# A hand-ordered Mamba, experts and attention kernel: new order times in the state loops, first convolution tap on ScalarE, a shorter row split

## The chip, the cores and the metric

The kernel runs on one NeuronCore of a Trainium2 chip. The metric is the time of one execution in microseconds (us) on the device; shorter is better. The time before is the median of three runs. Four layers are computed in one launch on 4 batches of 1024 tokens of 128 channels. The engines are PE (TensorE), DVE (VectorE), ACT (ScalarE), POOL (GpSimd) and SP, which here only issues transfers.

## What is computed

The reference, cut to the layers that the change touches. Two more layers follow, a differential attention and a layer of soft experts.

```python
x = x + _layernorm(_mamba_forward(_layernorm(x), ...))
x = x + _layernorm(_L0_ffn_ref(_layernorm(x), ...))
x = x + _layernorm(_L1_attn_ref(_layernorm(x), ...))
x = x + _layernorm(_L1_ffn_ref(_layernorm(x), ...))

def _mamba_forward(x, ...):                 # d_exp = 256, n = 16 states, dt rank 8
    u, z = split(x @ W_in.T)
    uc = silu(conv(u, taps=3) + conv_b)
    B_ssm, C_ssm, dt = split(uc @ W_xproj.T)
    delta = softplus(dt @ W_dt.T + b_dt)
    h = exp(delta * A) * h + (delta * uc) * B_ssm      # over time, for each of 16 states
    y = sum_n h * C_ssm + uc * D
    return (y * silu(z)) @ W_out.T

def _L0_ffn_ref(x, ...):                    # 8 experts, top 2, and one shared expert
    h = gelu(x @ W1[e] + b1[e]);  y = h @ W2[e] + b2[e]
    return sum over the top two of w * y  +  gelu(x @ sW1 + sb1) @ sW2 + sb2
```

## The kernel before

Every engine's program is written out in full, with semaphores between engines. Each engine runs its instructions strictly in the order in which they are written. That order is made by `weave`: each stream of work (state loop, front, middle, back, expert layer) is a Python generator that yields a planned time ahead of each piece, and the piece with the smallest time is emitted next. The times stand in tables (`IN_AT` for the front of a batch, `OUT_AT` for its back, `F_AT` for its expert layer) and in numbers in the loop functions. They set the order and nothing else; no instruction waits for a time.

Work on the 1024 tokens of a batch lies transposed: 256 inner channels as two halves c = 0, 1 of 128 partitions, time along the free dimension.

**The state loop** (`loop_dve`, `loop_act`, `loop_pe`, `loop_pool`) has 16 iterations per batch, one for each state n. This text calls iteration n of batch b "b.n". In one iteration:

- PE spreads row n of B over all partitions (L548 into `ps0`), later row n of C (into `ps1`).
- ACT makes `exp(delta * A)` for both halves (L451).
- DVE does six instructions of 1024 columns: two products with the B row (L328), the scans of c = 1 and of c = 0 (L334), two products with the C row (L340). The scan of c = 1 has one input in PSUM; that of c = 0 has both inputs in SBUF (`BIG`).
- POOL adds the two products to `yy` (L423, both inputs in SBUF). It starts when the first L340 is done.

**The front** of batch b+1 runs inside the loop of batch b: statistics (L306, L310), normalization (L315, eight instructions), transposes (L561) and the input product (L568) on PE, copies to `up` on ACT (L464), the convolution on DVE for each half (first tap L356, two more taps L360), SiLU on ACT (L469), the projection (L575, L473), the split of the projected rows into three bf16 parts (L366 to L376), softplus (L382, L384, L389, L392 with exponentials and logarithms on ACT), and `du` (L397). **The back** of batch b (gate L406, output product L603, statistics, normalization, addition to X by POOL at L437) runs inside the loop of batch b+1, and so does its **expert layer**: statistics and normalization, transposes (L768), the low part of the input (L659), gate logits (L757 to L759 with the small `gw`), top two (L634 to L668), weights (L671 to L681), and then 18 expert steps (9 experts on two halves of the tokens). A step is four groups "up" of three matmuls (L757 to L759) with a GELU each on ACT (L744), then "down" (L828, 32 records of 128 columns; with a bias product L826 for the shared expert), whose result DVE weighs and sums (L696, four instructions; `PLAN`'s shared expert is copied by ACT, L752). For batches 0 to 2 all "down" results go through one PSUM bank, so the next "down" waits until the last sum is done. The loop of batch 3 has no front in it; the back and the expert layer of batch 3 come after all loops.

ACT holds one table set of functions at a time: between the exponentials of the loop and the GELUs it runs an ACT_TABLE_LOAD.

After that come a barrier, the attention, a barrier, and the soft experts. The constants are loaded by SP at the start; ACT and DVE wait for all of them together (semaphore `s_c`).

## Time and profile before

| | us |
|---|---|
| median of 3 runs | 3073.71 (3073.69 to 3076.74) |
| the profiled execution | 3073.01 |
| its span, first to last instruction | 3070.9 |
| mean granted TensorE clock | 0.873 |
| busy: PE / DVE / ACT / POOL | 2391.0 / 2202.3 / 1696.2 / 1448.7 |
| start of the loop of batch 0, 1, 2, 3 (first L328) | 72.79 / 270.61 / 513.97 / 766.73 |
| end of the last loop; transposes of the last expert layer | 987.42 / 1027.21 |

The page gives busy shares over the whole span. To read a stage, one takes the start of an instruction that marks it (here the first L328 of each loop) and asks for the busy time of each engine between two such marks. A row "engine line <- engine line" names who ended a wait. In the rows that list groups of instructions, the mean length of one stands behind the busy time: the same instruction with two lengths has been held up in one of them.

### The profile page before, as it was taken

To read this page: it belongs to the slowest core of one execution; us is meant where nothing else is said; L and a number is where in the kernel's file an instruction comes from. 1 tells how busy PE (TensorE), PEld (TensorE's weight loads), DVE (VectorE), ACT (ScalarE), POOL (GpSimd) and SP (SyncE) were. 2 spreads that over 40 slices of the span, in tenths; PEclk is the share of its full clock that TensorE was granted. 3 is DMA by queue.
4 is the path that set the end of the run, shared out by engine and by line. 5 is a ranking of instruction groups with operands and counts; after the bars stand their busy time and mean duration, and the time that the engine had idled before them with its cause. 6 is when DMAs were issued, how large, how long until landed. Compare 5 with 4: busy or idle time off the path is not lost.

```text
span 3070.9 us, 42340 instructions
## 1 busy us (share of the span) xinstructions
PE 2391.0 (78%) x15570; PEld 1711.5 (56%) x15570; DVE 2202.3 (72%) x3693; ACT 1696.2 (55%) x2621; POOL 1448.7 (47%) x1343
## 2 busy tenths in 40 slices
PE   2333579388488794999999999999999478767987
PEld 0101256156256572777677777777777356745675
DVE  5999999989986314888788878887888543354334
ACT  5333476376474342878777877787777224222322
POOL 0434323433433102655866676667567541564156
PEclk7555699698798896999999999999999789887988
DMA  3000000000000001101000000000000100000000
GB/s 103 0 0 0 1 1 1 0 1 1 0 1 1 1 1 40 26 24 29 21 23 22 22 22 22 22 22 21 22 22 1 42 1 1 1 14 1 1 1 14
DMA packets 32031, 42.04 MB, mean 14 GB/s; under 512 B 8897, under 2 KB 18130, under 8 KB 31442
## 3 DMA queue, kind: packets, MB, share of 16 engines
...
## 4 chain that ended last, share of the span: by engine, by line
PE 49%; DVE 24%; issue 12%; POOL 9%; ACT 5%; SPq 1%; DMA 0%; POOLq 0%; DVEq 0%; ACTq 0%
PE ps L1073 10%; PE ps L1051 6%; PE ps L1062 6%; PE ps L828 5%; DVE MA L1209 3%; DVE lnb L315 2%; DVE BIG L340 2%; PE ps L757 2%; PE ps L1842 2%; PE ps L1033 2%; PE ps L759 2%; PE ps L758 2%; DVE BIG L334 2%; PE ps L1784 1%; DVE ps L328 1%
## 5 line engine op out<-in xcount | busy, mean ns | idle before, releaser
L1209 DVE TENSOR_REDUCE MA<-ps 128x1 f32<-128x1024 f32 x512 | 623.3, 1221 | 191.4 <-PE ps L1051 178.6
L423 POOL TENSOR_TENSOR MA<-MA,BIG 128x1024 f32<-128x1024 f32 x128 | 309.3, 2438 | 590.4 <-DVE BIG L340 559.1
L1073 PE MATMUL ps<-MA,WB 128*64 128x128 f32 x4096 | 504.4, 277 | 0.0
L1073 PEld LDWEIGHTS ps<-MA,WB 128*64 128x64 f32 x4096 | 442.6, 137 | 88.9 <-issue 87.9
L1051 PE MATMUL ps<-BIG 96*128 96x512 f16 x1024 | 313.8, 388 | 13.6 <-ACT WB L1136 5.0
L1136 ACT ACTIVATE WB<-ps,MA 128x1024 f32<-128x1024 f32 x206 | 229.7, 1115 | 149.2 <-DVE MA L1209 149.2
L828 PEld LDWEIGHTS ps<-WB,HR 128*128 128x128 f32 x2304 | 285.5, 199 | 32.5 <-issue 16.9
L828 PE MATMUL ps<-WB,HR 128*128 128x128 f32 x2304 | 295.5, 285 | 9.0 <-DVE acc L696 9.0
L744 ACT ACTIVATE HR<-ps,b 128x512 f32<-128x512 f32 x288 | 191.2, 687 | 174.1 <-PE ps L759 173.3
L1143 ACT ACTIVATE MA<-ps 128x1024 f32<-128x1024 f32 x256 | 259.9, 1015 | 5.0 <-PE ps L1062 5.0
L1605 POOL TENSOR_TENSOR BIG<-MA,BIG 128x512 f32<-128x512 f32 x128 | 132.2, 1049 | 232.3 <-PE ps L1828 74.5
L1266 POOL TENSOR_TENSOR MA<-MA 128x2 f32<-128x2 f32 x128 | 25.2, 197 | 366.7 <-DVE MA L1213 366.7
L451 ACT ACTIVATE BIG<-MA,aneg 128x1024 f32<-128x1024 f32 x128 | 141.3, 1143 | 100.7 <-DVE BIG L334 98.8
L1136 ACT ACTIVATE MA<-ps,MA 128x1024 f32<-128x1024 f32 x153 | 170.7, 1116 | 45.7 <-DVE MA L1209 45.5
L696 DVE SCALAR_TENSOR_TENSOR acc<-ps,g,acc 128x128 f32<-128x128 f32 x256 | 71.7, 342 | 159.7 <-PE ps L828 159.6
L548 PE MATMUL ps<-bc,sel 96*128 96x512 bf16 x128 | 54.8, 524 | 162.2 <-DVE BIG L334 104.4
L1062 PE MATMUL ps<-ident,WB 128*128 128x128 f32 x1232 | 166.7, 279 | 5.4 <-POOL WB L1278 2.6
L1062 PEld LDWEIGHTS ps<-ident,WB 128*128 128x128 f32 x1232 | 144.7, 144 | 44.0 <-DVE WB L1218 10.9
L757 PE MATMUL ps<-xT,WB 128*128 128x512 f16 x288 | 119.2, 414 | 48.4 <-ACT HR L744 42.9
L334 DVE TENSOR_TENSOR_SCAN BIG<-BIG,ps 128x1024 f32<-128x1024 f32 x64 | 146.2, 2284 | 5.3
L340 DVE TENSOR_TENSOR BIG<-BIG,ps 128x1024 f32<-128x1024 f32 x128 | 149.0, 1205 | 0.1
L334 DVE TENSOR_TENSOR_SCAN BIG<-BIG 128x1024 f32<-128x1024 f32 x64 | 146.5, 2289 | 0.0
(306 smaller groups left out, 5262.3 us busy)
## 6 DMA issues: line engine op xcount, KB each, us to landing
...
```

Of the source, the lines that this page charges most:

```text
L334: e.tensor_tensor_scan(db[k][c], da[k][c], db[k][c] if c == 0 else ps[0][:, :], 0.0, ALU.mult, ALU.add).then_inc(*v_mscan.up(b, n, c))
L340: e.tensor_tensor(db[k][c], db[k][c], ps[1][:, :], ALU.mult).then_inc(*v_mth.up(b, n, c))
L423: e.tensor_tensor(yy[:, c, :], yy[:, c, :], db[n % 2][c], ALU.add).then_inc(*p_my.up(b, n, c))
L744: e.activation(hr[(4 * k + f) % 8], bank[4 + f % 2], ACT.Gelu, bias=small["b1"][:, PLAN[k][1], f:f + 1], scale=BACK).then_inc(*a_fg.up(b, ...
L757: e.matmul(o, w[0], x[0], start=first, stop=False)
L828: i = e.matmul(o, hr[(4 * kk + f) % 8][:, 128 * j:128 * j + 128], w2[:, x, f, :], start=f == 0 and x != 8, stop=f == 3)
L1051: x = e.matmul(ps[s][:, 512 * h:512 * h + 512], stack[q % 2][0:96, 0, 2 * pp + s, 128 * i:128 * i + 128], stack[q % 2][0:96, 1, 2 * pp + s ...
L1062: x = e.transpose(ps[2][:, 128 * k:128 * k + 128], P_of(n, 0)[:, 128 * k:128 * k + 128], ident[:, :])
L1073: x = e.matmul(bank[6][64 * pp:64 * pp + 64, 0:128], V[(4 * b + g) % 2][:, k, 64 * pp:64 * pp + 64], DT[n % 2][:, 128 * k:128 * k + 128], ...
L1136: e.activation(P_of(n, s), ps[s][:, :], ACT.Exp, bias=L[:, 2 * s + pp:2 * s + pp + 1], scale=1.0, accum_out=L[:, 4 + 2 * s + pp:5 + 2 * s ...
L1143: e.activation(DT[n % 2], ps[2][:, :], ACT.Copy, scale=1.0).then_inc(*a_at.up(n))
L1209: e.tensor_reduce(L_of(n)[:, c:c + 1], ps[s][:, :], AX, ALU.max, negate=True).then_inc(*v_amx.up(n, s))
```

## The change

1. New numbers in the tables and in the loop functions (now `LOOP_AT`, `F_AT0`, `F_AT2`, `F_AT3`). They reorder the streams on all engines up to the end of the first expert layer.
2. The first tap of the convolution, with the bias, goes from DVE (L356) to ACT (an Identity activation with a scale and a bias for each partition), after the last copy to `up`.
3. The split of the projected rows writes straight into the rows that PE reads; each part is made on fewer partitions. Four DVE instructions take the place of six.
4. The load of `lnp` (four transfers) goes from the start to the beginning of the attention.
5. A way of weighing the experts on ACT and POOL is added, but `WEIGHTED = []` leaves it unused, so the sums stay on DVE.

```diff
-N_PERIOD, M_PERIOD, M_FIRST = 14.0, 224.0, 56.0
+N_PERIOD, M_PERIOD, M_FIRST = 13.11, 209.76, 56.0
+WEIGHTED = []
...
-IN_AT = {"stats": slot(4), "norm": slot(5), "tr": 82.5, "u": 87, "conv0": slot(6), "conv1": slot(7), "silu": 111.5,
+IN_AT = {"stats": 59.8, "norm": 72, "tr": 75, "u": 79.5, "tap0": 90.3, "tap1": 88, "conv0": 84.9, "conv1": 98,
...
+LOOP_AT = {"tb": 0.04, "scan1": 2.4, "scan0": 4.95, "th": 7.2, "add": 9.57, "da": 0.1, "rows0": 5.5, "rows1": 10.88,
+           "z": 20.8, "zK": 1.85, "za": 0.98}
...
-        for i in range(4):
-            consts += [(lnp[:, i, :], d["lnp"][i:i + 1, :].partition_broadcast(128)),
-                       (lam[:, i, :], d["lam"][i:i + 1, :].partition_broadcast(128))]
+        consts += [(lam[:, i, :], d["lam"][i:i + 1, :].partition_broadcast(128)) for i in range(4)]
...
             for c in range(2):
                 yield in_at(b, f"conv{c}")
-                e.wait_ge(*a_m.at("u", b, c, 1))
-                if c == b == 0:
-                    e.wait_ge(*p_const.at("pad"))
-                e.tensor_scalar(cv[c], u[:, c, 0:1024], cw[:, c, 0:1], cb[:, c:c + 1], ALU.mult, ALU.add).then_inc(
-                    *dve_own.up())
                 for k in (1, 2):
-                    e.wait_ge(*dve_own.now())
+                    if k == 1:
+                        e.wait_ge(*a_mtap.at(b, c))
+                    else:
+                        e.wait_ge(*dve_own.now())
...
-            e.tensor_copy(bc[0], r).then_inc(*dve_own.up())
+            e.tensor_copy(hi, r[0:96, :]).then_inc(*dve_own.up())
             e.wait_ge(*dve_own.now())
-            e.tensor_tensor(r, r, bc[0], ALU.subtract).then_inc(*dve_own.up())
+            e.tensor_tensor(r[0:64, :], r[0:64, :], hi[0:64, :], ALU.subtract).then_inc(*dve_own.up())
             e.wait_ge(*dve_own.now())
             yield in_at(b, "bc2")
-            e.tensor_copy(bc[1], r).then_inc(*dve_own.up())
+            e.tensor_copy(hi[0:64, :], r[0:64, :]).then_inc(*dve_own.up())
             e.wait_ge(*dve_own.now())
-            e.tensor_tensor(hi, r, bc[1], ALU.subtract).then_inc(*dve_own.up())
-            e.wait_ge(*dve_own.now())
-            e.tensor_copy(hi[32:64, :], bc[1][32:64, :])
-            e.tensor_copy(hi[0:32, :], bc[0][0:32, :]).then_inc(*v_mbc.up(b))
+            e.tensor_tensor(hi[0:32, :], r[0:32, :], hi[0:32, :], ALU.subtract).then_inc(*v_mbc.up(b))
...
+            for c in range(2):
+                yield in_at(b, f"tap{c}")
+                for h in range(2):
+                    e.wait_ge(*a_m.at("u", b, c, h))
+                if c == b == 0:
+                    e.wait_ge(*p_const.at("pad"))
+                if c and b:
+                    e.wait_ge(*v_mdl.at(b - 1, 0))
+                e.activation(cv[c], up[b % 2][:, c, 0:1024], ACT.Identity, bias=small["convb"][:, c:c + 1],
+                             scale=small["convw"][:, c, 0:1]).then_inc(*a_mtap.up(b, c))
...
+            for i in range(4):
+                e.dma_start(lnp[:, i, :], d["lnp"][i:i + 1, :].partition_broadcast(128)).then_inc(s_lnp, 16)
```

What the tables do is seen in the order of the instructions. First DVE in iterations 1.6 and 1.7, where the taps of batch 2 are taken. L334 is a scan, L340 the product with the C row, L696 the sum of an expert. The order before:

```order
L334 SCALAR_TENSOR_TENSOR BIG<-BIG 128x1024
L340 TENSOR_TENSOR BIG<-BIG,ps 128x1024 x2
L356 TENSOR_SCALAR lnb<-MA,convw,convb 128x1024
L360 SCALAR_TENSOR_TENSOR lnb<-MA,convw,lnb 128x1024 x2
L328 TENSOR_TENSOR BIG<-MA,ps 128x1024
L328 TENSOR_TENSOR ps<-MA,ps 128x1024
L334 SCALAR_TENSOR_TENSOR BIG<-BIG,ps 128x1024
L334 SCALAR_TENSOR_TENSOR BIG<-BIG 128x1024
L696 SCALAR_TENSOR_TENSOR acc<-ps,g,acc 128x128 x4
L340 TENSOR_TENSOR BIG<-BIG,ps 128x1024 x2
L356 TENSOR_SCALAR BIG<-MA,convw,convb 128x1024
L360 SCALAR_TENSOR_TENSOR BIG<-MA,convw,BIG 128x1024 x2
```

The taps stood behind the pair L340. The same place now, from the normalization in 1.5 on (L316 is L315 of before, L329 is L328, L335 is L334, L341 is L340, L359 is L360, L706 is L696):

```order
L316 TENSOR_SCALAR lnb<-X,st_m 128x128 x8
L341 TENSOR_TENSOR BIG<-BIG,ps 128x1024 x2
L329 TENSOR_TENSOR BIG<-MA,ps 128x1024
L329 TENSOR_TENSOR ps<-MA,ps 128x1024
L335 SCALAR_TENSOR_TENSOR BIG<-BIG,ps 128x1024
L706 SCALAR_TENSOR_TENSOR acc<-ps,g,acc 128x128 x4
L335 SCALAR_TENSOR_TENSOR BIG<-BIG 128x1024
L359 SCALAR_TENSOR_TENSOR lnb<-MA,convw,lnb 128x1024 x2
L341 TENSOR_TENSOR BIG<-BIG,ps 128x1024 x2
L706 SCALAR_TENSOR_TENSOR acc<-ps,g,acc 128x128 x4
```

The normalization and the taps now stand between the second scan and the pair of products; the other pieces of the fronts and backs moved in the same way. Second, ACT at the front of batch 2, where the first tap is now made (L762 is the GELU, L460 the copy to `up`, L470 the tap, L447 the exponentials of the loop):

```order
L447 ACT_TABLE_LOAD
L447 ACTIVATE BIG<-MA,aneg 128x1024 x2
L460 ACTIVATE MA<-ps 128x512 x2
L762 ACT_TABLE_LOAD
L762 ACTIVATE HR<-ps,b 128x512 x2
L460 ACTIVATE MA<-ps 128x512
L762 ACTIVATE HR<-ps,b 128x512 x2
L460 ACTIVATE MA<-ps 128x512
L470 ACTIVATE lnb<-MA,convb,convw 128x1024
L470 ACTIVATE BIG<-MA,convb,convw 128x1024
```

Both taps stand behind all four copies and four GELUs. Third, DVE after the last iteration, from the last pair of products to the transposes of the last expert layer. Before:

```order
L340 TENSOR_TENSOR BIG<-BIG,ps 128x1024 x2
L696 SCALAR_TENSOR_TENSOR acc<-ps,g,acc 128x128 x4
L406 TENSOR_TENSOR MA<-MA 128x1024 x2
L306 BN_STATS st_m<-lnb 128x6 x8
L310 BN_AGGR st_m<-st_m 128x2 x8
L696 SCALAR_TENSOR_TENSOR acc<-ps,g,acc 128x128 x4
L315 TENSOR_SCALAR lnb<-lnb,st_m 128x128 x8
L696 SCALAR_TENSOR_TENSOR acc<-ps,g,acc 128x128 x8
L306 BN_STATS st_f<-acc 128x6 x8
L310 BN_AGGR st_f<-st_f 128x2 x8
L315 TENSOR_SCALAR lnb<-acc,st_f 128x128 x8
L306 BN_STATS st_f<-X 128x6 x8
```

And now (L402 is the gate):

```order
L341 TENSOR_TENSOR BIG<-BIG,ps 128x1024 x2
L706 SCALAR_TENSOR_TENSOR acc<-ps,g,acc 128x128 x4
L402 TENSOR_TENSOR MA<-MA 128x1024 x2
L706 SCALAR_TENSOR_TENSOR acc<-ps,g,acc 128x128 x4
L307 BN_STATS st_f<-acc 128x6 x8
L311 BN_AGGR st_f<-st_f 128x2 x8
L316 TENSOR_SCALAR lnb<-acc,st_f 128x128 x8
L307 BN_STATS st_m<-lnb 128x6 x8
L311 BN_AGGR st_m<-st_m 128x2 x8
L316 TENSOR_SCALAR lnb<-lnb,st_m 128x128 x8
L307 BN_STATS st_f<-X 128x6 x8
```

Two expert sums instead of four stand behind the loop, and the closing of the expert layer of batch 2 stands ahead of the closing of batch 3's Mamba layer.

## Rows read from the trace of the kernel before

**Rows 1.** Stretches (loops 0 to 3, transition): length; PE, PEld, DVE, ACT, POOL busy; clock.
```profile
72.79:270.61 197.82, 61.96 (x102) 13.94 (x102) 194.45 (x143) 68.01 (x70) 76.87 (x33) 0.52 0.00 0
270.61:513.97 243.36, 170.15 (x869) 104.40 (x870) 224.13 (x284) 139.53 (x162) 88.89 (x40) 0.78 0.00 1
513.97:766.73 252.76, 178.32 (x986) 113.67 (x985) 232.36 (x319) 150.93 (x175) 92.17 (x43) 0.83 0.00 1
766.73:987.42 220.69, 161.02 (x946) 106.52 (x945) 187.86 (x269) 123.31 (x143) 86.07 (x41) 0.83 0.00 1
987.42:1027.21 39.79, 21.00 (x155) 16.65 (x154) 20.04 (x90) 6.29 (x10) 14.05 (x10) 0.88 0.00 1
```

**Rows 2.** DVE in order of time: start, length; one bare iteration, 0.0.
```profile
72.79 1.22 DVE L328 TENSOR_TENSOR BIG<-MA,ps 128x1024 f32<-128x1024 f32 x1
...
81.88 1.21 DVE L328 TENSOR_TENSOR BIG<-MA,ps 128x1024 f32<-128x1024 f32 x1
```

**Rows 3.** POOL's adds and what stands beside them on DVE, by time.
```profile
345.35 4.65 POOL L423 TENSOR_TENSOR MA<-MA,BIG 128x1024 f32<-128x1024 f32 x2 [8.38 <-DVE BIG L340]
...
346.32 5.30 DVE L315 TENSOR_SCALAR lnb<-X,st_m 128x128 f32<-128x128 f32 x8
...
286.62 3.57 DVE L334 TENSOR_TENSOR_SCAN BIG<-BIG 128x1024 f32<-128x1024 f32 x1
```

**Rows 4.** DVE by group in the four loops, 73 to 987: busy, mean of one.
```profile
L392 DVE SCALAR_TENSOR_TENSOR MA<-MA,lnb 128x1024 f32<-128x1024 f32 x6 | 19.5, 3254 | 0.2
L315 DVE TENSOR_SCALAR lnb<-X,st_m 128x128 f32<-128x128 f32 x24 | 15.9, 730 | 0.0
L360 DVE SCALAR_TENSOR_TENSOR BIG<-MA,convw,BIG 128x1024 f32<-128x1024 f32 x6 | 13.6, 2270 | 0.2
...
L315 DVE TENSOR_SCALAR lnb<-X,st_f 128x128 f32<-128x128 f32 x24 | 6.4, 339 | 0.0
...
L356 DVE TENSOR_SCALAR BIG<-MA,convw,convb 128x1024 f32<-128x1024 f32 x3 | 5.8, 1934 | 0.0
...
L356 DVE TENSOR_SCALAR lnb<-MA,convw,convb 128x1024 f32<-128x1024 f32 x3 | 2.8, 929 | 7.6 <-ACT MA L464 7.6
...
L375 DVE COPY rows<-bc 32x1024 bf16<-32x1024 bf16 x2 | 0.8, 417 | 0.1
```

**Rows 5.** The same instructions with POOL at rest, DVE before the loops.
```profile
33.74 2.61 DVE L360 SCALAR_TENSOR_TENSOR lnb<-MA,convw,lnb 128x1024 f32<-128x1024 f32 x2
...
69.26 1.22 DVE L392 SCALAR_TENSOR_TENSOR MA<-MA,lnb 128x1024 f32<-128x1024 f32 x1
```

**Rows 6.** DVE's waits in the four loops: total, times, longest.
```profile
DVE acc L696 <- PE ps L828: 50.4, 19, 9.1
DVE lnb L356 <- ACT MA L464: 7.6, 3, 3.6
DVE bc L366 <- ACT lnb L473: 5.2, 3, 2.7
```

**Rows 7.** PE and the pace of the experts, by time.
```profile
407.26 0.38 PE L757 MATMUL ps<-xT,WB 128*128 128x512 f16 x1
407.48 0.38 PE L758 MATMUL ps<-xT,WB 128*128 128x512 f16 x1
...
410.16 3.73 PE L828 MATMUL ps<-WB,HR 128*128 128x128 f32 x32
...
937.90 2.08 PE L828 MATMUL ps<-WB,HR 128*128 128x128 f32 x8
...
1068.38 1.12 DVE L696 SCALAR_TENSOR_TENSOR acc<-ps,g,acc 128x128 f32<-128x128 f32 x4 [5.34 <-PE ps L828]
```

**Rows 8.** ACT by group in the loops.
```profile
L501 ACT ACTIVATE MA<-MA,dcol 128x1024 f32<-128x1024 f32 x8 | 9.0, 1147 | 13.7 <-DVE MA L406 13.7
```

**Rows 9.** The start, and the transition after the last loop.
```profile
18.30 0.23 ACT L264 ACTIVATE aneg<-alog 128x32 f32<-128x32 f32 x1 [16.30 <-DMA gts<-gates_dram]
...
1027.21 1.97 PE L768 MATMUL ps<-ident,lnb 128*128 128x128 f32 x8 [14.42 <-DVE lnb L315]
```

More of the change, by code:

```diff
@@ L121, in f_at @@
 def f_at(b, what, more=0.0, k=0):
-    f = F_AT if b < NB - 1 else F_AT3
-    return out_at(b, "x") + 4 + f[what] + more + (k * f["K"] if k else 0)
+    f = F_AT[b]
+    return out_at(b, "x") + 3.2 + f[what] + more + (k * f["K"] if k else 0)
 def program(nc, d, out):
@@ L330, in loop_dve @@
                 for c in (1, 0):
[L331 removed]
+                    yield l_at(b, n, LOOP_AT[f"scan{c}"])
                     e.wait_ge(*a_mda.at(b, n, c))
@@ L745, in experts0_act @@
                                      scale=BACK).then_inc(*a_fg.up(b, k, f))
+                if k >= 1 and PLAN[k - 1][1] != 8 and b in WEIGHTED:
+                    yield done_at(b, k - 1)
+                    h, x = PLAN[k - 1]
+                    e.wait_ge(*t_fdn.at(b, k - 1))
+                    if k == 2:
+                        e.wait_ge(*v_fc.at(b))
+                    prev = [j for j in routed if j < k - 1][-1:]
+                    if prev:
+                        e.wait_ge(*p_fcb.at(b, prev[0]))
+                    elif b - 1 in WEIGHTED:
+                        e.wait_ge(*p_fcb.at(b - 1, 17))
+                    for j in range(4):
+                        i = e.activation(weighted[:, j, :], down(b, k - 1)[:, 128 * j:128 * j + 128], ACT.Identity, bias=0.0,
+                                         scale=G6[:, 4 * h + j, x:x + 1])
+                    i.then_inc(*a_fcb.up(b, k - 1))
                 if k >= 1 and PLAN[k - 1][1] == 8:
```

81 lines of the change are left out of this document (49 added, 32 removed).

## The prediction, made before the changed kernel ran

> **What bounds the kernel now.** I read the stage table first. It cuts the first third into the four state loops and what follows [rows 1]. In loops 0 to 2 DVE is busy 194, 224 and 232 us of 198, 243 and 253, so DVE sets their length; PE is busy 70% in loops 1 and 2. In loop 3 DVE is busy 188 of 221 and the experts of PE share the bound. A DVE iteration with nothing else in it takes 81.88 - 72.79 = 9.09 us [rows 2], so 64 of them are 582 of the 915 us of the loops. The rest is pieces of fronts and backs, waits, and stalls inside instructions.
>
> The stalls are the point of this change. POOL's two adds last 4.65 us and start when the first L340 is done. A normalization behind the pair L340 starts one microsecond later and takes 5.30 us [rows 3]; eight of its instructions at the free length of 339 ns [rows 4] would take 2.1. L392 takes 3254 ns in the loops and 1.22 us with POOL at rest, L360 on `BIG` 2270 ns and 1.30 [rows 4, 5]. The bare instructions of the loop with an input in PSUM (L328, L340) keep their length beside POOL.
>
> **Part 1, the stalls.** For each group on DVE I take (mean in the loops - free length) x count. L392: 6 x 2.03 = 12.2. L315: 24 x 0.391 = 9.4 for the row shown, 13.4 for its two other slow groups. L360: 6 x 0.97 = 5.8 [rows 4, 5]. The same sum over the other pieces that stand behind L340 (L384 6.1, L389 7.4, L366 to L373 14.7, L382 3.7, L360 on `lnb` 1.8) gives 33.7. Together 74.5 us. Afterwards these pieces stand between the second scan and the pair L340. POOL started behind the first L340 and needs 4.65; the second L340, two L328 and the scan of c = 1 last 1.16 + 2.25 + 2.20 = 5.6, so POOL rests from then until the next first L340. Value -74.5. Ends: -75, and -60 if every place where POOL's pair comes late stalls once. These late places are few: after the gate in 1.0, 2.0 and 3.0 (POOL waits for ACT's start of `yy`), after the normalizations of 1.2, 2.1, 2.2 and their like, where an addition to X or a root stands ahead of the pair. What such a place costs stands in the trace: the scan with two SBUF inputs after the gate took 3.57 us instead of 2.27 [rows 3].
>
> The Trainium skill ("SBUF — State Buffer", section "Who interferes with whom") says that a VectorE instruction with two SBUF inputs, or in a two-port mode, and a GpSimd instruction that reads SBUF exclude each other for a whole instruction, and that whoever starts first wins. The trace agrees [rows 3]. By this rule the new order is itself exposed: the scan of c = 0 has no piece ahead of it any more that takes the blow, and 0.9 us is all that parts it from POOL's pair. At some dozen late places with 1.3 us each the sum would be 15 us worse; the end of -60 from the rows covers that.
>
> **Part 2, the tap.** DVE loses 5.8 + 2.8 = 8.6 us in the loops [rows 4]. ACT gains 8 instructions of about 1.15 us, the length of an Identity with a scale for each partition and 1024 columns; that row shows no table load for its line [rows 8]. ACT is busy 57 to 60% in loops 1 and 2 [rows 1], so its time is hidden, but not its place: the convolution now waits for ACT (part 4). Value -8.6.
>
> **Part 3, the row split.** Two copies of 417 ns less for each front; the other four keep their length, since fewer partitions do not shorten an instruction. Six in the loops: -2.5 [rows 4]. The end if partitions counted is -5.
>
> **Part 4, the waits that come in place.** DVE now waits 50.4 + 7.6 + 5.2 = 63.2 us in the loops [rows 6]. They can't shrink with the stalls, since PE's experts have to be fed in the same stretch. An expert step at full clock takes PE 12 x 0.217 for "up" (407.48 - 407.26) and some 3.6 for "down" (32 records in 3.73, less the drain), 6.2 us; the undisturbed pace of the last expert layer is 5.34 + 1.13 = 6.47 [rows 7]. Eighteen steps (112) with the rows, transposes, and products of a front and a back (29) are 141 us of PE at full clock. They stand in 12 iterations, for which DVE needs 12 x 9.09 + 45 = 154 us without a stall. Before, they took about 189: loop 2 with its 253 us [rows 1] less the four iterations without experts (36 bare, 5 for the two products of the gate logits and the low part, 18 for statistics and normalizations, 5 of stalls). So DVE still sets the length, but with 8% to spare, and wherever the two fixed orders disagree one waits.
>
> I walked both orders by hand through loop 1 with these lengths. From the end of the expert weights in 1.4, DVE comes to the first `L360` after two L328, two scans, the normalization, the pair L340, two L328, a scan, an expert sum, a scan: 18.8 us. PE has to do 12 "up" groups (7.8), the shared "down" (4.6), one "down" (3.6), 16 transposes (3.2), four input products (3.6), three rows (1.3), some 2 for GELUs: 26; then a copy and the tap on ACT, 1.9. DVE waits 9 us there, 4 at the sum and 5 at the tap. In 1.8 three waits add up to 7. In 1.12 a sum stands late, and PE needs 4.6 + 2.6 + 3.6 + 0.9 = 11.7 us from it to the next sum, DVE 6.5: 5. Two more sums come to 2. About 4 us are new in 1.3 and 1.4: the low part of the input comes right behind the pair L340, 2.3 us after the normalization that PE and ACT first have to turn, and the weights stand beside POOL. That is 27, with small gaps 29, where DVE was idle 243.4 - 224.1 = 19.2 [rows 1]: +10. Loop 2 also has two sums in a row in 2.0, with a "down" of 3.6 between them: +13. Loop 3 (idle 32.8 now) has more expert steps in it: +5. Loop 0 loses 1 of its 3.4. A half-clock spell more (8 records took 2.08 us at 938, a quarter of 3.73 at 410 [rows 7]): +1. Together +28. Ends: 0 to +50.
>
> **Part 5, the ends.** After the last loop 39.8 us pass until the last expert layer starts on PE, with DVE busy 20 [rows 1, 9]. Two of its four expert sums, and one of the output product's waits behind "down", go; the chain that is left (POOL's pair 4.7, gate 2.3, product and copy 4.5, statistics, root and normalization twice at 6.5, addition 2.4, latencies 1 to 2) is 28 us, but two experts more are squeezed into loop 3. -10, ends -14 and 0. The start: ACT's wait for the constants ends at 18.3 us [rows 9]; four transfers less, issued every 0.4 us, are -1.6, the two copies in the first front -0.8, and the taps on ACT ahead of the SiLU +0.6. -2, ends -3 and 0.
>
> **Sum.** 3073.0 (the profiled execution, 0.7 below the median of the runs) - 74.5 - 8.6 - 2.5 + 28 - 10 - 2 = 3003.4. Loop by loop: 198 becomes 171, 243 becomes 227, 253 becomes 239, 221 stays near 220.
>
> **Rivals.**
> A. PE keeps up. Nothing but DVE's work counts and the waits stay at 63: 3003 - 28 = 2975. For it: PE's 141 us fit in DVE's 154, and the undisturbed pace of 6.47 shows that nothing else slows a step. Against it: the walk, and that those 12 iterations now take 189 us while PE has 141 of work in them.
> B. PE and the GELUs behind the exponentials already set the experts' iterations. Then these 12 iterations keep their 189 us twice; only loop 0 (-27), the start of loop 1 (-15), the four iterations without experts in loop 2 (-11) gain, and the ends (-2): 3073 - 55 = 3018; with loop 3 longer by the two added experts, 3030. For it: DVE's largest wait is for "down". Against it: DVE is busy 92% in loop 1.
> C. POOL's rest is not where the order puts it, so the stalls only move. Then parts 2, 3 and the ends remain: 3073 - 8.6 - 2.5 - 2 = 3060. Against it: 5.6 us cover 4.65.
> D. Slower. The waits of part 4 let TensorE fall to half clock. A step then takes twice its 6.2 us, as the 8 records at 938 do. Loops 1 to 3 hold 54 steps; PE has about 30 us to spare in each of the first two, so from (70 + 60) / 6.2 = 21 more slow steps on the gain of 70 is gone, and at 25 the time is 3073 + 25 = 3098. The clock now is 0.78 to 0.83 in these loops [rows 1], so about four tenths of their time are slow already, most of it where PE has nothing to do. Against it: PE becomes denser, not sparser.
> The Trainium skill ("TensorE: Matmul & The Clock Gate", section "HAM oscillation — how this bites in real kernels") says that waits between bursts of matmuls send TensorE back to half clock and that each burst then starts slow. The spell at 938, behind a wait, agrees; by that rule alone D would be the case, but the same rule spares a PE that is fuller than before.
>
> **Chances.** Forecast (2988 to 3018) 0.50, A 0.20, B 0.20, C 0.03, D 0.03, and 0.04 for something unread. The predicted time is 3003. The range 2968 to 3034 takes in A and B with the ends of the unknown costs and leaves out C, D and the tails of A. A measurement of this kernel can tell about 0.2% (6 us) from no change. Faster by more than that 0.95, within it 0.02, slower 0.03.
>
> **What would show it.** Right: L392 near 1.22 us, L315 near 0.34 everywhere, iteration 0.5 at 11.1 us (9.09 and a normalization of 2.03); DVE's waits in the loops near 91 us, with one for the tap of about 5 us in 1.6 and 2.6; 28 to 32 us from the last loop to the last expert layer. Wrong: long scans of c = 0 (part 1), no wait at the tap (A), experts' iterations of 189 us in sum (B), L392 still above 2 us (C), a granted clock below 0.7 in loops 1 and 2 (D).

## The result and the profile after

The changed kernel takes 3019.1 us (median of 4, 3018.1 to 3021.2), the one before 3073.7 beside it: a ratio of 0.982, with an interval of 0.981 to 0.984. It is 55 us faster; 70 were forecast. The profiled execution took 3018.3 us, its span is 3015.9.

The stage table of the kernel after, cut at the first L329 of each loop and at the transposes of the last expert layer; it answers [rows 1], with loop 3 and the transition in one row. Columns: stretch, length, PE, PEld, DVE, ACT and POOL busy, granted clock.

```profile
70.82:249.14 178.32, 59.23 (x102) 13.39 (x102) 167.59 (x138) 72.89 (x74) 72.81 (x33) 0.53 0.00 0
249.14:489.50 240.36, 175.81 (x936) 109.13 (x936) 199.77 (x284) 153.31 (x178) 82.82 (x40) 0.83 0.00 1
489.50:734.95 245.45, 183.07 (x984) 116.16 (x984) 205.95 (x316) 154.81 (x180) 87.06 (x43) 0.83 0.00 1
734.95:972.23 237.28, 167.74 (x1030) 113.90 (x1030) 199.61 (x355) 124.84 (x146) 99.24 (x50) 0.85 0.00 1
```

I split each length into what DVE does and what it idles (length minus busy). The two rows of before for loop 3 and the transition [rows 1] are added up.

| us | loop 0 | loop 1 | loop 2 | loop 3 and transition | sum |
|---|---|---|---|---|---|
| length before | 197.8 | 243.4 | 252.8 | 260.5 | 954.4 |
| length forecast | 171 | 227 | 239 | 250 | 887 |
| length after | 178.3 | 240.4 | 245.5 | 237.3 | 901.4 |
| DVE busy before, after | 194.5, 167.6 | 224.1, 199.8 | 232.4, 206.0 | 207.9, 199.6 | 858.8, 772.9 |
| DVE idle before, after | 3.4, 10.7 | 19.2, 40.6 | 20.4, 39.5 | 52.6, 37.7 | 95.6, 128.5 |

DVE's work fell by 85.9 us, where the forecast has 74.5 + 8.6 + 2.5 = 85.6. The idle time rose by 32.9, where it has 28 - 10 = 18. That is the whole miss, and it has two signs: in loops 0 to 2 the idle time rose by 48 us where -1 + 10 + 13 = 22 were forecast, and in loop 3 with the transition it fell by 15 where 5 - 10 = -5 was forecast. The stretch after the transposes is unchanged: 2043.7 us before (3070.9 - 1027.21), 2043.7 after.

The groups of DVE from 71 to 942 of the kernel after, which answer [rows 4]. Columns behind the shapes: count, busy time, mean ns of one, idle time ahead of them.

```profile
L359 DVE SCALAR_TENSOR_TENSOR lnb<-MA,convw,lnb 128x1024 f32<-128x1024 f32 x6 | 7.7, 1284 | 19.5 <-ACT lnb L470 19.4
L359 DVE SCALAR_TENSOR_TENSOR BIG<-MA,convw,BIG 128x1024 f32<-128x1024 f32 x6 | 7.6, 1271 | 0.1
L388 DVE SCALAR_TENSOR_TENSOR MA<-MA,lnb 128x1024 f32<-128x1024 f32 x6 | 7.4, 1226 | 0.2
...
L316 DVE TENSOR_SCALAR lnb<-X,st_m 128x128 f32<-128x128 f32 x24 | 6.4, 339 | 0.0
...
L679 DVE TENSOR_SCALAR g<-g 128x8 f32<-128x8 f32 x3 | 4.4, 1480 | 0.0
```

The large groups stand at their free lengths: L388 (L392 of before) at 1226 ns instead of 3254, L359 on `BIG` at 1271 instead of 2270, L316 at 339 instead of 730. Only the small expert weights (L679) now fall beside POOL, at 1480 ns instead of the 579 of L671 before (160 in b_pair_late below). In place of the stalls stands a new wait of 19.4 us for L470, the tap on ACT. The waits of DVE up to the transposes (total, times, longest). [rows 6] covers the loops alone; up to the transposes the kernel before has 55.5 us in 22 waits for L828:

```profile
DVE acc L706 <- PE ps L861: 72.4, 27, 6.4
DVE lnb L359 <- ACT lnb L470: 19.4, 3, 7.9
DVE BIG L329 <- PE ps L554: 7.7, 2, 4.6
```

Iteration 1.6 shows what the new waits are made of. DVE, in order of time (start, length; in brackets the wait and who ended it):

```profile
334.88 1.12 DVE L706 SCALAR_TENSOR_TENSOR acc<-ps,g,acc 128x128 f32<-128x128 f32 x4 [5.08 <-PE ps L861]
335.92 2.28 DVE L335 TENSOR_TENSOR_SCAN BIG<-BIG 128x1024 f32<-128x1024 f32 x1
343.92 2.60 DVE L359 SCALAR_TENSOR_TENSOR lnb<-MA,convw,lnb 128x1024 f32<-128x1024 f32 x2 [5.72 <-ACT lnb L470]
346.44 2.35 DVE L341 TENSOR_TENSOR BIG<-BIG,ps 128x1024 f32<-128x1024 f32 x2
```

ACT at the same time:

```profile
337.14 0.60 ACT L460 ACTIVATE MA<-ps 128x512 f32<-128x512 f32 x1 [1.22 <-PE ps L574]
337.76 1.28 ACT L762 ACT_TABLE_LOAD   x1
339.05 1.27 ACT L762 ACTIVATE HR<-ps,b 128x512 f32<-128x512 f32 x2
340.21 0.60 ACT L460 ACTIVATE MA<-ps 128x512 f32<-128x512 f32 x1
340.69 1.30 ACT L762 ACTIVATE HR<-ps,b 128x512 f32<-128x512 f32 x2
342.16 0.60 ACT L460 ACTIVATE MA<-ps 128x512 f32<-128x512 f32 x1 [0.17 <-PE ps L574]
342.65 1.23 ACT L470 ACTIVATE lnb<-MA,convb,convw 128x1024 f32<-128x1024 f32 x1
343.79 1.24 ACT L470 ACTIVATE BIG<-MA,convb,convw 128x1024 f32<-128x1024 f32 x1
...
350.91 0.69 ACT L762 ACTIVATE HR<-ps,b 128x512 f32<-128x512 f32 x1 [5.88 <-PE ps L792]
```

And PE:

```profile
348.84 0.74 PE L554 MATMUL ps<-rows,sel 96*128 96x512 bf16 x2 [3.15 <-DVE BIG L341]
...
357.15 0.61 PE L790 MATMUL ps<-xT,WB 128*128 128x512 f16 x1 [4.08 <-ACT HR L762]
```

DVE waits 5.7 us for the tap on `lnb`, though both copies to `up` that this tap reads ended at 337.7 (the third and the fourth copy are for the other half, and four GELUs stand between them). While DVE waits, the pair L341 is late, and with it the C row L554, which overwrites the bank that L341 reads. PE's queue stands behind L554 for 3.15 us, ACT then waits 5.88 us for the "up" group behind it, and PE 4.08 us for a GELU. A wait is passed round three engines. The last of the three waits has a second cause: between that GELU and the one before it ACT runs a table load, the two exponentials of the loop and another table load (351.61 to 356.41).

The end of the change, DVE from the last pair of products on:

```profile
942.26 1.12 DVE L706 SCALAR_TENSOR_TENSOR acc<-ps,g,acc 128x128 f32<-128x128 f32 x4
946.10 2.36 DVE L402 TENSOR_TENSOR MA<-MA 128x1024 f32<-128x1024 f32 x2 [2.71 <-POOL MA L419]
948.80 1.13 DVE L706 SCALAR_TENSOR_TENSOR acc<-ps,g,acc 128x128 f32<-128x128 f32 x4 [0.34 <-PE ps L861]
```

Two sums stand behind the last loop. PE's transposes start at 972.23, 29.9 us after the loop's last product (942.35); before it was 39.8.

### The profile page after: what moved, and what is told of

Same layout as the page of the kernel before. It is cut to its first block, busy times and chain, and to the rows that moved or that the text cites. A ratio compares the mean times of both kernels' runs of the same rounds, so it can differ in the third digit from the quotient of the medians.

```text
span 3015.9 us, 42357 instructions
## 1 busy us (share of the span) xinstructions
PE 2384.5 (79%) x15570; PEld 1709.3 (57%) x15570; DVE 2112.3 (70%) x3677; ACT 1715.5 (57%) x2639; POOL 1430.0 (47%) x1343
## 4 chain that ended last, share of the span: by engine, by line
PE 53%; DVE 19%; issue 10%; POOL 9%; ACT 8%; SPq 1%; DMA 0%; POOLq 0%; DVEq 0%; ACTq 0%
PE ps L1109 10%; PE ps L861 6%; PE ps L1087 6%; PE ps L1098 6%; DVE MA L1245 3%; PE ps L790 2%; PE ps L792 2%; PE ps L791 2%; PE ps L1069 2%; ACT HR L762 2%; PE ps L1879 2%; DVE lnb L316 2%; DVE BIG L341 2%; POOL MA L419 1%; PE ps L1821 1%
## 5 line engine op out<-in xcount | busy, mean ns | idle before, releaser
L419 POOL TENSOR_TENSOR MA<-MA,BIG 128x1024 f32<-128x1024 f32 x128 | 299.0, 2357 | 557.7 <-DVE BIG L341 535.0
L762 ACT ACTIVATE HR<-ps,b 128x512 f32<-128x512 f32 x288 | 190.8, 687 | 170.9 <-PE ps L792 170.0
L1302 POOL TENSOR_TENSOR MA<-MA 128x2 f32<-128x2 f32 x128 | 25.2, 197 | 370.7 <-DVE MA L1249 370.7
L706 DVE SCALAR_TENSOR_TENSOR acc<-ps,g,acc 128x128 f32<-128x128 f32 x256 | 71.9, 344 | 176.4 <-PE ps L861 176.1
L554 PE MATMUL ps<-bc,sel 96*128 96x512 bf16 x128 | 55.4, 530 | 147.2 <-DVE BIG L335 72.3
L1098 PEld LDWEIGHTS ps<-ident,WB 128*128 128x128 f32 x1232 | 143.7, 143 | 44.7 <-DVE WB L1254 10.3
L447 ACT ACTIVATE BIG<-MA,aneg 128x1024 f32<-128x1024 f32 x128 | 140.9, 1143 | 36.6 <-DVE BIG L335 34.8
L335 DVE TENSOR_TENSOR_SCAN BIG<-BIG,ps 128x1024 f32<-128x1024 f32 x64 | 146.1, 2283 | 5.4
L341 DVE TENSOR_TENSOR BIG<-BIG,ps 128x1024 f32<-128x1024 f32 x128 | 149.5, 1210 | 0.1
L335 DVE TENSOR_TENSOR_SCAN BIG<-BIG 128x1024 f32<-128x1024 f32 x64 | 145.3, 2270 | 0.0
```

The costliest lines, as they stand in the source:

```text
L335: e.tensor_tensor_scan(db[k][c], da[k][c], db[k][c] if c == 0 else ps[0][:, :], 0.0, ALU.mult, ALU.add).then_inc(*v_mscan.up(b, n, c))
L341: e.tensor_tensor(db[k][c], db[k][c], ps[1][:, :], ALU.mult).then_inc(*v_mth.up(b, n, c))
L419: e.tensor_tensor(yy[:, c, :], yy[:, c, :], db[n % 2][c], ALU.add).then_inc(*p_my.up(b, n, c))
L762: e.activation(hr[(4 * k + f) % 8], bank[4 + f % 2], ACT.Gelu, bias=small["b1"][:, PLAN[k][1], f:f + 1], scale=BACK).then_inc(*a_fg.up(b, ...
L1098: x = e.transpose(ps[2][:, 128 * k:128 * k + 128], P_of(n, 0)[:, 128 * k:128 * k + 128], ident[:, :])
```

## The experiments

Times of different groups of runs are compared by their ratio to the kernel before, which ran beside each of them (3067 to 3071 us). The kernel after was run again beside the last three.

> The kernel after itself, unchanged, beside the three other runs of this group, to compare them on one chip. 3012 to 3020 where the kernel before takes 3067 to 3074.

It came out at 0.9819, where its first runs had 0.9823.

| run | ratio to before (interval) | loops 0, 1, 2; loop 3 with transition |
|---|---|---|
| after, again | 0.9819 (0.9803 to 0.9834) | 178.3, 241.1, 245.4; 237.6 |
| b_pair_late | 0.9849 (0.9832 to 0.9867) | 177.4, 228.4, 238.9; 261.6 |
| a_pair_early | 1.0092 (1.0062 to 1.0123) | 201.6, 258.7, 264.9; 249.0 |
| a_half_down | 0.9663 (0.9646 to 0.9679) | 180.0, 230.7, 239.2; 235.4 |
| a_two_taps | 0.9820 (0.9799 to 0.9842) | 176.2, 243.7, 243.2; 236.0 |
| a_rowC_late | 0.9801 (0.9783 to 0.9819) | 177.1, 238.2, 239.8; 235.7 |
| a_rows_late | 0.9785 (0.9769 to 0.9802) | 179.1, 235.2, 237.0; 236.0 |
| a_tap_dve | 0.9774 (0.9758 to 0.9790) | 175.4, 233.8, 241.9; 237.4 |
| a_tap_own | 0.9808 (0.9787 to 0.9828) | 172.9, 236.9, 246.4; 236.1 |
| a_both | 0.9779 (0.9763 to 0.9795) | 174.0, 235.1, 240.2; 236.0 |
| a_ends | 0.9839 (0.9823 to 0.9855) | 177.9, 237.5, 245.1; 240.7 |
| a_k_late | 0.9858 (0.9838 to 0.9878) | 180.1, 239.8, 245.0; 247.5 |

### b_pair_late: the kernel before, with the pair behind the pieces

```diff
-                yield l_at(b, n, 7.2)
+                yield l_at(b, n, 13.9)
...
-                        yield l_at(b, n - 1, 10) if b + n else in_at(0, "du", 1)
+                        yield l_at(b, n - 1, 13.95) if b + n else in_at(0, "du", 1)
```

> The kernel before, with only the place of the pair L340 changed: its planned time goes from 7.2 to 13.9 of each period of 14 (and the C row on PE from 10 to 13.95), so that the pieces that stood behind the pair now stand ahead of it. Tap, row split, transfers and all tables of before stay. Theory 1 (the stalls beside POOL are the gain, and the fixed orders of DVE and PE give part of it back as waits): L392 falls from 3254 to about 1220 ns, L315 to 339, DVE's busy time in the four loops falls by 60 to 75 us, its waits rise by 25 to 45, time 3073 - 65 + 35 = about 3043 (3030 to 3055). Rival C (POOL's rest is not there, stalls only move): busy time in the loops unchanged, 3065 to 3080. Rival B (PE and the GELUs set the experts' iterations): busy time falls as in theory 1, but only loop 0 and the iterations without experts gain, 3045 to 3055 or more; loop 0 about -20.

Measured: 3023.4 us, 46 less than before by the ratio. Two numbers give five sixths of the whole change. In loops 1 and 2 they give more than the whole: 228.4 and 238.9 us, where the kernel after takes 240.4 and 245.5; what the kernel after has over this one lies in loop 3, the transition and the start. The groups of DVE in its four loops:

```profile
L392 DVE SCALAR_TENSOR_TENSOR MA<-MA,lnb 128x1024 f32<-128x1024 f32 x6 | 7.4, 1226 | 0.2
L315 DVE TENSOR_SCALAR lnb<-X,st_m 128x128 f32<-128x128 f32 x24 | 6.3, 338 | 0.0
...
L356 DVE TENSOR_SCALAR lnb<-MA,convw,convb 128x1024 f32<-128x1024 f32 x3 | 2.4, 812 | 8.5 <-ACT MA L464 8.5
L356 DVE TENSOR_SCALAR BIG<-MA,convw,convb 128x1024 f32<-128x1024 f32 x3 | 2.4, 797 | 0.0
```

DVE's busy time up to the last transposes is 776.2 us, 82.6 less than before (858.8), with no tap and no copy taken away; its idle time is 130.2, 34.6 more. Besides the pieces of part 1 (74.5) and the tap's stalls (3.8), the gate's weights (L671 from 579 to 160 ns, L675 from 792 to 176, three of each) and the scans of c = 0 (2289 to 2268 ns) add 4.4. Rival C falls. The gain was a little more than theory 1 gave it (0.9849 of the first 3073.7 is 3027, against 3030 to 3055), and rival B's 3045 or more did not come. Loops 1 and 2 came out within 2 us of the lengths that the forecast has for the whole change (227 and 239). Loop 3 with its transition did not move (260.5, now 261.6). The two rows on L356 say what the tap costs DVE with POOL at rest: 0.80 us, 4.8 for the six in the loops. The other 3.8 of their 8.6 [rows 4] were stalls.

### a_pair_early: the kernel after, with the pair ahead of the pieces again

```diff
-LOOP_AT = {"tb": 0.04, "scan1": 2.4, "scan0": 4.95, "th": 7.2, "add": 9.57, "da": 0.1, "rows0": 5.5, "rows1": 10.88,
+LOOP_AT = {"tb": 0.04, "scan1": 2.4, "scan0": 4.95, "th": 4.96, "add": 9.57, "da": 0.1, "rows0": 5.5, "rows1": 10.88,
```

> The kernel after, with only the planned time of the pair L341 moved from 7.2 to 4.96, so that the pieces stand behind the pair again; all else of the change stays. Theory 1: L388 back to about 3.2 us, L316 to 0.7, DVE's busy time in the loops up by 60 to 75, its waits down by 30 to 45, time 3019 + 30 = about 3050 (3040 to 3060). Rival C: no change, 3019. Rival A (waits do not answer to stalls): 3019 + 70 = 3090.

Measured: 3097.9 us, 28 slower than the kernel before and 84 slower than the kernel after. The direction held, the size did not: it is beyond the 3090 of the case in which the waits do not answer to the stalls. Its groups of DVE in the loops:

```profile
L388 DVE SCALAR_TENSOR_TENSOR MA<-MA,lnb 128x1024 f32<-128x1024 f32 x6 | 19.5, 3254 | 0.2
L393 DVE TENSOR_TENSOR MA<-MA 128x1024 f32<-128x1024 f32 x7 | 18.5, 2670 | 0.0
L359 DVE SCALAR_TENSOR_TENSOR BIG<-MA,convw,BIG 128x1024 f32<-128x1024 f32 x6 | 17.1, 2858 | 0.1
```

L388 is back at 3254 ns, the value of before to the nanosecond. L393 (`du`) was free in the kernel before (L397, 1209 ns) and now takes 2670, since the new tables put it right behind the pair. So the busy time rose by 94.6 us, more than the 60 to 75 expected, and the waits fell by only 21.8 (30 to 45 expected): the waits do answer to the stalls, by a quarter of them. An undo in other surroundings does not have to give back what the edit gave.

### a_half_down and a_two_taps: is it PE's work or DVE's work?

```diff
-                        for f in range(4):
+                        for f in (0, 3):
                             i = e.matmul(o, hr[(4 * kk + f) % 8][:, 128 * j:128 * j + 128], w2[:, x, f, :],
```

> The kernel after, with two of the four matmuls of each block of 'down' left out in the first expert layer (f = 1 and 2), so that this part of the experts' sum is not computed: 16 records instead of 32, about 1.8 us of PE less for each step, everything else and both orders unchanged. If PE's amount of work sets the experts' iterations (rival B), loops 1 and 2 fall by 10 to 25 us each and most of DVE's 28 us of waits for 'down' in each of them goes. If DVE sets them and the waits are places where the two fixed orders disagree (forecast), loops 1 and 2 fall by 3 to 8 each, the wait for the tap stays. The last expert layer (some 14 steps after the loops, pace 6.47 us) falls by 10 to 25 in both cases and is read apart.

The kernel leaves out half of the experts' second product in the first expert layer. Measured: PE's busy time falls by 23.8 and 23.9 us in loops 1 and 2, the loops by 9.7 and 6.2. Behind the transposes, where the last expert layer stands, it is 40 us (2960.1 - 956.3 = 2003.9 against 2043.7), more than expected. DVE's wait for "down" in these two loops fell from 55.5 to 34.5 us, its waits for the tap rose from 11.4 to 14.0. Loop 1 touches rival B's lower end, loop 2 lies in the forecast's range. Both are well under half of the work that was taken away: PE's amount of work has a part in the length, but does not set it. The edit does not take work away alone: the granted clock of both loops fell from 0.83 to 0.79.

The other side, a_two_taps, leaves out the third tap of the convolution, so its result is incomplete too:

```diff
-                for k in (1, 2):
+                for k in (1,):
```

> The kernel after, with the third tap of the convolution left out (k = 2), so that the convolution is not complete: one DVE instruction of 1.27 us less for each half of each front, 6 in the loops, 8 in all. If DVE's work sets the length everywhere, loops 0, 1 and 2 fall by 2.5 us each and the whole by 10. If PE sets the experts' iterations, loop 0 falls by 2.5, loops 1 and 2 by under 1 each, and the waits behind the convolution grow by what was taken away; the whole falls by 4 to 6.

Measured: no difference from the kernel after that could be told (0.9820), where one case had 10 us and the other 4 to 6. Loop 0 falls by 2.1 and loop 2 by 2.2 of the 2.6 us taken away. Loop 1 grows by 3.3, and that is one iteration. Iteration 1.8 in the kernel after, and in this run:

```profile
365.77:391.23 25.46, 21.27 (x105) 12.15 (x105) 13.26 (x17) 17.54 (x22) 4.68 (x2) 0.93 0.00 0
```

```profile
362.05:392.68 30.63, 27.16 (x105) 14.51 (x105) 13.25 (x17) 17.57 (x22) 4.65 (x2) 0.72 0.00 0
```

The same 105 matmuls, but the granted clock is 0.72 instead of 0.93: PE stood at 1.2 GHz, the lower of its two levels, through most of it. It begins behind a wait of PE:

```profile
372.92 3.74 PE L578 MATMUL ps<-MA,wx 128*104 128x512 f32 x4 [3.33 <-ACT lnb L476]
...
386.65 4.95 PE L858 MATMUL ps<-WB,HR 128*128 128x128 f32 x32
```

The 32 records of "down" take 4.95 us here, 3.73 at full clock [rows 7]. So loop 1 says nothing on the tap. a_tap_own has such a spell in 2.8 (30.6 us at a clock of 0.72, where the kernel after has 25.2; loop 2 there is 1 us longer at 0.81).

### a_tap_dve and a_tap_own: what the tap on ACT costs

a_tap_dve is the kernel after with the tap back on DVE, at the place of the second tap; `a_mtap` and the tap of `front_act` are gone.

```diff
+                e.wait_ge(*a_m.at("u", b, c, 1))
...
+                e.tensor_scalar(cv[c], u[:, c, 0:1024], cw[:, c, 0:1], cb[:, c:c + 1], ALU.mult, ALU.add).then_inc(
+                    *dve_own.up())
                 for k in (1, 2):
-                    if k == 1:
-                        e.wait_ge(*a_mtap.at(b, c))
-                    else:
-                        e.wait_ge(*dve_own.now())
+                    e.wait_ge(*dve_own.now())
```

> The kernel after, with the first tap of the convolution back on DVE and gone from ACT; all tables stay. Forecast: DVE's busy time up by 6 times 0.80 (the tap's length in the run with the late pair, where POOL rests) = 4.8 us in the loops, not the 8.6 of the old kernel, since 3.8 of these were stalls; DVE's wait ahead of the convolution (19.4 us) falls by 3 times 1.2 to 2.4 because ACT's tap no longer lies in the chain, so the whole moves by -3 to +3 us of 3019. If the tap on ACT were worth its 8.6 us, 3028.

Measured: 3000.8 us, 0.9774 against 0.9819: about 14 us faster than the kernel after, outside every case. This is the main finding. DVE in iteration 1.6 of this run, to be held against the rows above:

```profile
330.21 1.12 DVE L698 SCALAR_TENSOR_TENSOR acc<-ps,g,acc 128x128 f32<-128x128 f32 x4 [4.73 <-PE ps L853]
331.26 2.28 DVE L335 TENSOR_TENSOR_SCAN BIG<-BIG 128x1024 f32<-128x1024 f32 x1
333.45 0.79 DVE L357 TENSOR_SCALAR lnb<-MA,convw,convb 128x1024 f32<-128x1024 f32 x1
334.28 2.61 DVE L361 SCALAR_TENSOR_TENSOR lnb<-MA,convw,lnb 128x1024 f32<-128x1024 f32 x2
336.80 2.35 DVE L341 TENSOR_TENSOR BIG<-BIG,ps 128x1024 f32<-128x1024 f32 x2
341.06 1.13 DVE L698 SCALAR_TENSOR_TENSOR acc<-ps,g,acc 128x128 f32<-128x128 f32 x4 [1.92 <-PE ps L853]
```

The convolution follows the scan without a wait. Its taps wait 1.3 us in the loops, once, where the kernel after has 19.4, since the DVE tap needs two copies and no GELU. DVE is busy 4.9 us more (777.8 against 772.9) and idles 17.8 less (110.7 against 128.5). Even ahead of the loops the tap on ACT costs: the first L359 of the kernel after starts at 35.62, this kernel's tap at 32.06, and the loops start at 68.99 instead of 70.82. Loops 0, 1 and 2 are 2.9, 6.5 and 3.6 us shorter. Loops 1 and 2 (233.8 and 241.9) are still 5.4 and 3.0 us longer than in b_pair_late, which has the old tables: the new order of the other streams costs there too, and no run takes that apart.

a_tap_own keeps the tap on ACT and moves it up:

```diff
-            for c in range(2):
-                yield in_at(b, f"tap{c}")
+                yield in_at(b, "u", 1.05 + (2 if b else 0.9) * (2 * c + 1))
```

> The kernel after, with each tap on ACT right behind the two copies that it needs instead of behind all four. DVE's wait ahead of the convolution (7.9 us in loop 0, 5.7 in loops 1 and 2) falls to 1 to 4 each. If the waits stand in a row on one chain, the next one grows by as much and the time falls by 3 to 8 us; if they are independent it falls by 10 to 14.

Measured: 0.9808. The wait at the tap fell from 19.4 to 4.4 us, the time by some 3 us (the intervals overlap). Loop 0, with no experts in it, took 5.4 of the 7.9 it had waited; loops 1 and 2 together 2.5 of 11.4, the spell in 2.8 included. So most of a wait that goes comes back elsewhere. How much of the 14 us is the tap's place in ACT's queue, and how much that it stands between the copies and the convolution with 1.24 us at all, these two runs don't separate: the transposes start 7.7 us earlier than in the kernel after (14.7 with the tap on DVE), with a spell of some 5 us in it.

### a_rowC_late, a_rows_late and a_both: PE behind the rows

```diff
-LOOP_AT = {"tb": 0.04, "scan1": 2.4, "scan0": 4.95, "th": 7.2, "add": 9.57, "da": 0.1, "rows0": 5.5, "rows1": 10.88,
+LOOP_AT = {"tb": 0.04, "scan1": 2.4, "scan0": 4.95, "th": 7.2, "add": 9.57, "da": 0.1, "rows0": 9.0, "rows1": 15.0,
```

The first of the two runs has only `rows1` moved.

> The kernel after, with only the place of the C row on PE moved: planned time 15.0 of a period of 13.11 instead of 10.88, so that more expert, front and back work of PE stands ahead of the row product that waits for DVE's pair L341. The first four runs leave this theory (the mutual wait): the waits that came in place of the stalls are not a lack of PE time but the row products, behind which PE's queue stands still while DVE works or waits; in the kernel after PE waits 49 us at L554 for L341 and 36 us for the scan L335 in loops 1 to 3, then the GELUs and the sums come late. It expects the wait for L341 to fall below 25 us, DVE's wait for 'down' by 10 to 25 us, loops 1 and 2 down by 4 to 10 us each: 3000 to 3012. Rival (the chain of GELUs and exponentials on ACT, with their table loads, sets these iterations): the wait moves to another instruction of PE and the time stays within 4 us of 3019. Slower (3025 or more) if the late C row makes the pair itself wait.

> As the run before, and the B row on PE moved from 5.5 to 9.0 as well. The mutual wait expects a further fall of 2 to 8 us, 2995 to 3008, with the wait for L335 below 25 us; the rival on ACT expects 3015 to 3023. If DVE then waits at L329 for its row (7.7 us in the kernel after), the fall is given back there.

Measured: 0.9801 and 0.9785, some 6 and 10 us less than the kernel after (the interval of the first overlaps with the one of the kernel after). With the C row alone late, PE's wait for L341 falls to 23.9 us, as expected, but DVE's wait for "down" only to 64.9 and loops 1 and 2 by 2.2 and 5.6. PE's waits between 248 and 945 of the kernel after:

```profile
PE ps L554 <- DVE BIG L341: 49.0, 15, 5.7
PE ps L790 <- ACT HR L762: 43.3, 28, 5.5
PE ps L554 <- DVE BIG L335: 35.7, 10, 5.6
```

And in a_rows_late:

```profile
PE ps L790 <- ACT HR L762: 43.1, 29, 5.0
PE ps L554 <- DVE BIG L335: 34.4, 9, 5.6
PE ps L554 <- DVE BIG L341: 27.0, 8, 5.7
PE ps L822 <- DVE g L689: 27.0, 3, 10.3
```

With both rows late the wait for L341 nearly halves, and DVE's wait for "down" falls from 72.4 to 48.3 us. Against the expectation the wait for L335 stays at 34.4, DVE's own wait for its B row grows from 7.7 to 22.9 us, and PE waits 27.0 instead of 9.7 at the transposes of the expert weights (L822). With the same 984 to 986 matmuls in loop 2, before, after, b_pair_late, a_pair_early, a_rowC_late and a_rows_late take 252.8, 245.5, 238.9, 264.9, 239.8 and 237.0 us for it. The order moves the length where the work does not.

a_both has the rows late and the tap on DVE.

> The kernel after with the first tap back on DVE, and with the row products of the loop later on PE (B row 9.0, C row 15.0). The two edits alone gave about 15 and 12 us (in the ratio to the kernel before). If they act on different waits (the tap's chain on ACT; PE standing behind the rows) they add up: 27 us, 2987 to 2995. If both only give PE's queue the same slack, the second is worth little: 2998 to 3004.

Measured: 3001.8 us, 0.9779, the same as the tap on DVE alone. The two edits do not add. DVE's wait for "down" falls from 71.3 to 53.7 us against the tap on DVE alone, but its wait for the B row rises from 7.9 to 23.0; that both edits relieve the same ring of waits is the reading of this, not a test of it. DVE is busy 201 of 235 and 207 of 240 us in loops 1 and 2. What holds the last 33 us in each was not tested; PE's waits for the GELUs (44.7 us here, 41.0 already in the kernel before, 31.8 in b_pair_late) are a candidate.

### a_ends and a_k_late: the transition

```diff
-OUT_AT3 = {"gate": 0.5, "yy": 0.33, "out": 3, "stats": 8.92, "rstd": 14.45, "norm": 12.08, "x": 13}
+OUT_AT3 = {"gate": 0.5, "yy": 0, "out": 3, "stats": 5.5, "rstd": 8.5, "norm": 10.5, "x": 13}
```

(`F_AT3` goes back to its old numbers with it.)

> The kernel after with the tables of the last back and the last expert layer as before (OUT_AT3, F_AT3): the statistics of batch 3's Mamba output stand again ahead of the last expert sum and of the closing of batch 2's expert layer. If this order carries the gain between the last loop and the last expert layer, the transition grows by 4 to 8 us; if the gain is that fewer expert sums stand behind the loop, by 0 to 2.

```diff
-         "cT": 26.6, "k": 18, "K": 8.28, "up": 0.8, "dn": 4, "dnj": 1, "ge": 0.7, "done": 9.95, "add": 1.4,
-         "end": 170.5, "rnorm": 176.5, "x": 179.8}
+         "cT": 26.6, "k": 32, "K": 8.28, "up": 0.8, "dn": 4, "dnj": 1, "ge": 0.7, "done": 9.95, "add": 1.4,
+         "end": 184.5, "rnorm": 190.5, "x": 193.8}
```

> The kernel after with the expert steps of batch 2 planned 14 later (k from 18 to 32, and the end of that layer), as far behind the start of the loop as in the kernel before, so that about two of its sums stand behind the last loop again. Seen from the forecast: loop 3 gets shorter by 3 to 6 us and the transition longer by 8 to 12, whole +4 to +8. If the early start of the steps costs loop 3 nothing, only the transition grows: +10 to +14. If it does not matter where the two sums stand: within 2.

Measured beside the kernel after (237.6 us from the start of loop 3 to the transposes, 207.6 of them in loop 3): a_ends 240.7, all of it in the transition (33.2 against 30.0), between its two cases. a_k_late 247.5: the transition 34.5 instead of 30.0, and loop 3 213.0 instead of 207.6, where the forecast's view had it 3 to 6 shorter. The whole is some 12 us longer (0.9858 against 0.9819), as the second case has it. Starting batch 2's experts earlier shortens both, so it was wrong that two experts more had to be paid for in loop 3.

## Why the prediction came out as it did

**Part 1, the stalls: right.** L392, L315 and L360 fell to the lengths named, iteration 0.5 to 11.1 us, and the pieces moved alone took 82.6 us of work off DVE (the sum's 74.5, the 3.8 that sat in the tap, and 4.4 of groups that the sum left out). The few late places cost little. The Trainium skill ("SBUF — State Buffer", section "Who interferes with whom") says that a VectorE instruction with two SBUF inputs and a GpSimd instruction that reads SBUF exclude each other for a whole instruction. The runs agree in both directions: 3254 ns becomes 1226 and, in a_pair_early, 3254 again. The dozen exposed scans, for which the text set aside 15 us beside the sum, didn't come: the scans of c = 0 take 2270 ns on average in the loops of the kernel after.

**Part 2, the tap: the step that failed.** I took -8.6 from DVE and said of ACT that "its time is hidden, but not its place". Both halves were off. Of the 8.6 us, 3.8 were stalls that go with the pair moved alone; free, it is 6 x 0.80 = 4.8. And the tap on ACT cost more than the time saved: 17.8 us of DVE idle time and 1.8 at the start. I did walk to a wait of 5 us at the tap in 1.6 (5.72 measured) and booked it under part 4, without setting it against the kernel that has the tap on DVE. There the wait in 1.6 is nil. The tap is worth +14 us where the sum has -8.6.

**Part 3, the row split: right, by its rows.** No run undoes it alone, but with POOL at rest the six instructions take 13.9 us in the loops of b_pair_late and the four 11.3 in the kernel after. The length does not go by partitions: 1213 ns on 32 (L372), 1225 on 128 (L380). The books close: 858.8 - 82.6 (pair) - 4.8 (tap) - 2.5 gives 768.9 for DVE's work, 772.9 were measured, and the 4.0 left is L679, at 1480 ns where b_pair_late has 160 (3 x 1.32).

**Part 4, the waits: right in kind, short in size.** Forecast +28, of which loops 0, 1, 2 were -1, +10, +13; measured +7.4, +21.4, +19.1. DVE's waits in the loops are 108 us, where the sign had 91. In iteration 1.6 the walk came close (9 us, measured 5.08 + 5.72). What it missed: the tap's wait in loop 0 (7.9), where I saw no experts and expected no wait, and that a late pair holds up the C row, PE and then the GELUs. I priced waits one by one along two queues; here they run round three. With the tap on DVE the idle time is 110.7 us, 15.1 above before, against 18 in the sum. That looks like a hit and is in part luck: loops 0 to 2 idle 30 us more than before (22 forecast), loop 3 with the transition 15 less (5 forecast). The tap on ACT is 18 of the 26 us by which loops 0 to 2 idle more than forecast (48 against 22). The rest of the new order has a share too: b_pair_late runs loops 1 and 2 in 467.3 us, the tap on DVE in 475.7 and the kernel after in 485.8.

**Part 5, the ends: half right.** The start is -2.0 as forecast and the transition -9.9 against -10. Loop 3 was to "stay near 220" and took 207.4. Its five more microseconds of waits didn't come; its work fell by 6.0 and its idle time from 32.8 to 25.5. In the kernel before, one place of loop 3 (3.13) holds 13.6 us of them. DVE of the kernel before, by time:

```profile
943.59 1.22 DVE L328 TENSOR_TENSOR BIG<-MA,ps 128x1024 f32<-128x1024 f32 x1 [4.49 <-PE ps L548]
...
957.43 1.13 DVE L696 SCALAR_TENSOR_TENSOR acc<-ps,g,acc 128x128 f32<-128x128 f32 x4 [9.09 <-PE ps L828]
```

That iteration takes 23.5 us before, 24.4 with the pair alone moved, and 15.2 in the kernel after. It was in the trace, and I had not asked which of loop 3's waits the new start of the experts would dissolve. By a_k_late that start is worth 5.4 of loop 3's 13.3 us.

**The rivals.** B gave 3018 to 3030, the time is 3019, and the sign that the prediction named for it came: the twelve iterations with experts did not get shorter. Batch 0's in the kernel before (1.6 to 2.1), in b_pair_late (the same) and in the kernel after (1.5 to 2.0), columns as in the stage table:

```profile
352.68:541.37 188.69, 162.06 (x920) 108.14 (x920) 168.42 (x178) 132.43 (x155) 58.90 (x24) 0.91 0.00 1
325.65:504.92 179.27, 156.97 (x920) 105.12 (x920) 151.37 (x177) 130.94 (x155) 56.26 (x25) 0.95 0.00 1
313.80:505.39 191.59, 159.86 (x916) 107.85 (x916) 151.47 (x182) 128.20 (x151) 56.72 (x25) 0.92 0.00 1
```

Batch 1's take 188.5, 179.4 and 190.1 us. So as a description of where the kernel after gains nothing, B is right for loops 1 and 2, and the forecast is not. As a cause it falls: if PE and the GELUs set these iterations, b_pair_late could not do the same matmuls and GELUs in 9 us less. With the tap on DVE they take 185.1 and 186.6, with both rows late 186.1 and 181.7; with half of "down" gone only a quarter to two fifths of PE's relief reached loops 1 and 2, and loop 2 takes anything from 237 to 265 us with the same matmuls. The order holds them at 190. That B's number came out is luck for B: it had loop 0 at -27, as the forecast has, and measured are -19.5. A's waits of 63 us were far off. C fell with the first row of part 1. D's half-clock spells exist (one of them costs some 5 us), but the granted clock of loops 1 and 2 rose or held (0.78 and 0.83 before, 0.83 and 0.83 after). Behind its wait of 3.33 us PE starts slow in iteration 1.8 of a_two_taps. The Trainium skill ("TensorE: Matmul & The Clock Gate", section "HAM oscillation — how this bites in real kernels") says that a burst behind a wait starts slow, and this row agrees; the same wait of PE in the kernel after (3.34 us at 376.64) was followed by a short spell only.
